# Causal attention scores taken in 512-column pieces through two single PSUM banks by turns

## The reference

```
for i in range(H):                                  # 16 heads, one after the other
    att = jnp.einsum('btd,bsd->bts', q_rot, k_rot) * scale
    if cascade_bias is not None:
        att = att + cascade_w[i - 1] * cascade_bias
    att = jnp.where(causal, -jnp.inf, att)
    att = jax.nn.softmax(att, axis=-1)
    head_outputs.append(jnp.einsum('bts,bsd->btd', att, v[:, i]))
    cascade_bias = jnp.mean(att, axis=1, keepdims=True)
```

## Time and profile before

| | |
|---|---|
| time, median of 3 runs | 3336.99 us (3334.38 to 3339.17) |
| span of the profiled execution | 3451.7 us |
| ACT busy | 3085.3 us, 89% of the span |
| PE busy | 3126.0 us, 91% |
| DVE busy | 2614.4 us, 76% |
| POOL busy | 2147.9 us, 62% |
| first and last "take" on DVE | 46.9 and 3215.3 us |

### The profile page before, as it was taken

One profiled execution on the slowest core, in us unless ns is written; L12 is line 12 of the kernel. 1 busy time (PEld: TensorE's weight loads), 2 busy tenths in 40 slices (PEclk: granted clock), 3 DMA queues, 4 the chain that ended last, 5 costly groups with the idle time before them and its releaser, 6 DMA issues. The chain is left out here.

```text
span 3451.7 us, 93100 instructions
## 1 busy us (share of the span) xinstructions
PE 3126.0 (91%) x29688; PEld 1529.3 (44%) x29688; DVE 2614.4 (76%) x7854; ACT 3085.3 (89%) x8904; POOL 2147.9 (62%) x6194
## 2 busy tenths in 40 slices
PE   6899999989999989998999999998999998898955
PEld 3333333333444434454445444444444543444644
DVE  7666666666877787887888887787888877777754
ACT  4999999999999999998999999998999999888724
POOL 5666666665666367776666677775667655565345
PEclk9999999999999999999999999999999999999986
DMA  5322322232333324343444423344434333344353
GB/s 162 97 86 72 88 71 71 74 88 79 90 101 107 103 78 127 117 122 109 131 115 124 120 84 94 114 116 131 117 93 123 113 101 84 105 121 145 110 187 125
DMA packets 270525, 370.74 MB, mean 107 GB/s; under 512 B 61654, under 2 KB 177118, under 8 KB 270033
## 3 DMA queue, kind: packets, MB, share of 16 engines
q1 hardware_dynamic: 254784, 326.39, 32.4%
q0 software_dynamic: 14976, 37.34, 3.7%
q10 hardware_dynamic: 272, 1.05, 0.1%
HBM read 259.76 MB, written 104.40 MB: 106 GB/s over the span
## 5 line engine op out<-in xcount | busy, mean ns | idle before, releaser
L1490 DVE CUSTOM_DVE_ANT_0 att_a<-scores,window 128x128 f32<-128x128 f32 (+7 forms) x2048 | 1489.6, 754 | 464.9 <-PE scores L1182 307.7
L1356 ACT ACTIVATE att_a<-att_a,neg_max 128x128 f32<-128x128 f32 (+7 forms) x2048 | 1593.0, 778 | 73.3 <-DVE neg_max L1490 69.5
L1366 ACT ACTIVATE att_t<-scores 128x1024 f32<-128x1024 f32 (+7 forms) x2048 | 1329.5, 649 | 88.6 <-PE scores L1200 61.1
L1198 PE MATMUL scores<-q_stack,k_stack 104*128 104x512 bf16 (+3 forms) x3072 | 822.5, 333 | 130.1 <-DVE neg_max L1490 74.7
L1216 PE MATMUL pv<-att_t,v_sb 128*32 128x256 f32 (+7 forms) x16384 | 917.9, 300 | 5.7 <-ACT att_t L1366 3.3
L1182 PE MATMUL scores<-k_stack,q_stack 99*128 99x512 bf16 (+3 forms) x3072 | 687.7, 331 | 67.1 <-ACT att_t L1366 39.1
L1216 PEld LDWEIGHTS pv<-att_t,v_sb 128*32 128x32 f32 x16384 | 328.9, 108 | 592.9 <-issue 549.0
L1198 PEld LDWEIGHTS scores<-q_stack,k_stack 104*128 104x128 bf16 x3072 | 258.4, 98 | 531.2 <-DVE neg_max L1490 233.9
L1200 PE MATMUL scores<-identb,mask 128*128 128x128 bf16 x2048 | 454.7, 222 | 0.0
L1816 POOL TENSOR_SCALAR biasv<-col_sum,w_cas 128x8 f32<-128x8 f32 x240 | 88.8, 370 | 552.9 <-ACT att_t L1366 540.2
L1366 ACT ACTIVATION_READ_ACCUMULATOR att_t<-scores 128x1 f32 x2048 | 424.0, 207 | 0.0
(11 more groups left out here) (345 smaller groups left out, 4342.8 us busy)
## 6 DMA issues: line engine op xcount, KB each, us to landing
runner_r<-in_experts SPq DMA_DIRECT2D x137, 384.0 KB
qk_parts<-of_proj SPq DMA_DIRECT2D x128, 384.0 KB
of_proj<-in_xt SPq DMA_DIRECT2D x29, 1024.0 KB
q_stack<-qk_parts SPq DMA_DIRECT2D x256, 96.0 KB
k_stack<-qk_parts SPq DMA_DIRECT2D x256, 96.0 KB
q_stack<-qk_parts SPq DMA_DIRECT2D x256, 64.0 KB
k_stack<-qk_parts SPq DMA_DIRECT2D x256, 64.0 KB
head_out<-o_sb SPq DMA_DIRECT2D x252, 64.0 KB
```

The source lines that it names most:

```text
L1198: engine.matmul(scores[:, c0:c1], ks[0:ROWS_B, j * P:(j + 1) * P], qs[0:ROWS_B, j * P + c0 - base:j * P + c1 - base], start=True, stop=True)
L1356: engine.activation(taken, taken, EXP, scale=-1.0, bias=neg_max[:, n, i:i + 1], accum_out=row_sum[:, n, i:i + 1]).then_inc(s_exp_a, 1)
L1366: engine.activation(att_t[:, ring:ring + end - base], scores[:, base:end], EXP, accum_out=col_sum[:, n, j:j + 1]).then_inc(s_exp_b, 1)
L1490: engine.tensor_tensor_reduce(out=att_a[:, ring:ring + end - base], in0=scores[:, base:end], in1=window[:, T - (end - base):T], op0=ALU.ad ...
```

## The change

Pass A's rows go through banks 0 and 1 only, in pieces of at most 512 columns that use the two banks by turns. For each pair of blocks (short p, long p+1) there are three pieces: the first 512 columns of the long block, the short block, the rest of the long block. So a unit has 12 pieces (`NP`) where it had 8 blocks. A long block's second piece starts its minimum from the first's result (`scalar=least`), for which DVE waits on its own semaphore. Pass B's short blocks have bank 4 alone, so both cross waits go, in the program and in the planner.

```
+    PIECES, LAST_PIECE = [], {}
+    for p_ in range(0, TB, 2):
+        short_, long_ = A_LONG[p_], A_LONG[p_ + 1]
+        PIECES += [(p_ + 1, 0, WB), (p_, 0, short_), (p_ + 1, WB, long_)]
+        LAST_PIECE[p_], LAST_PIECE[p_ + 1] = len(PIECES) - 2, len(PIECES) - 1
+    NP = len(PIECES)
...
             if kind == "take":
-                busy = cols_a(key[1]) * 1.0417e-3 + 0.078
+                busy = cols_piece(key[1]) * 1.0417e-3 + 0.078
...
-                if p % 2 == 0 and block(x_ - 2, p - 1) >= 0:
-                    yield "exp_b", of_block(block(x_ - 2, p - 1))
...
-                if p % 2:
-                    yield "take", of_block(min(block(u + 2, p - 1), BLOCKS - 1))
...
+        def piece_room(c):
+
+            width = PIECES[c][2] - PIECES[c][1]
+            return scores[:, c % 2 * WB:c % 2 * WB + width]
...
-                pe.wait_ge(s_max, blocks_done(u, p - 2))
-                if p % 2 == 0:
-                    pe.wait_ge(s_exp_b, blocks_done(u - 2, p - 1))
-                for c0 in range(base, end, WB):
-                    c1 = min(end, c0 + WB)
-                    made = engine.matmul(scores[:, c0:c1], qs[0:ROWS_A, i * P:(i + 1) * P],
-                                         ks[0:ROWS_A, c0 - base:c1 - base], start=True, stop=True)
-                made.then_inc(s_a_filled, 1)
+                pe.wait_ge(s_max, pieces_done(u, c - 2))
+                engine.matmul(piece_room(c), qs[0:ROWS_A, i * P:(i + 1) * P], ks[0:ROWS_A, low:high],
+                              start=True, stop=True).then_inc(s_a_filled, 1)
...
                 pe.wait_ge(s_exp_b, blocks_done(u, p - 2))
-                if p % 2:
-                    pe.wait_ge(s_max, blocks_done(u + 2, p - 1))
...
-                dve.wait_ge(s_a_filled, u * TB + p + 1)
+                dve.wait_ge(s_a_filled, pieces_done(u, c))
                 dve.wait_ge(s_exp_a, u * TB + p + 1 - NEG)
+                if low:
+                    dve.wait_ge(s_max, pieces_done(u, c - 2))
                 engine.tensor_tensor_reduce(
-                    out=att_a[:, ring:ring + end - base], in0=scores[:, base:end], in1=window[:, T - (end - base):T],
-                    op0=ALU.add, op1=ALU.min, scale=-1.0, scalar=BIG, accum_out=neg_max[:, n, i:i + 1]).then_inc(s_max, 1)
+                    out=att_a[:, ring + low:ring + high], in0=piece_room(c), in1=window[:, T - A_LONG[p] + low:T - A_LONG[p] + high],
+                    op0=ALU.add, op1=ALU.min, scale=-1.0, scalar=least if low else BIG, accum_out=least).then_inc(s_max, 1)
```

More of the change, by code:

```diff
@@ L317, in cols_a, with cols_piece @@
             return A_LONG[p]
+        def cols_piece(c):
+            return PIECES[c][2] - PIECES[c][1]
         def cols_b(p):
@@ L324, in work @@
             if kind == "fill_a":
-                busy = cols_a(key[1]) * 0.42e-3 + 0.01
+                busy = cols_piece(key[1]) * 0.42e-3 + 0.01
                 return busy, busy + 0.165
@@ L370, in timetable @@
         blocks = [(u, p) for u in range(UNITS) for p in range(TB)]
+        pieces = [(u, c) for u in range(UNITS) for c in range(NP)]
         queues = {
             "ACT": [main],
-            "PE": [[("fill_a", k) for k in blocks], [("fill_b", k) for k in blocks], [("pv", k) for k in blocks],
+            "PE": [[("fill_a", k) for k in pieces], [("fill_b", k) for k in blocks], [("pv", k) for k in blocks],
                    [("rows", x_) for x_ in range(1, UNITS + 1)]],
-            "DVE": [[("take", k) for k in blocks], [("rows_copy", x_) for x_ in range(1, UNITS + 1)],
+            "DVE": [[("take", k) for k in pieces], [("rows_copy", x_) for x_ in range(1, UNITS + 1)],
                     [("o_move", u) for u in range(UNITS)]],
@@ L384, in needs @@
             if kind == "fill_a":
-                x_, p = key
-                if block(*key) >= 2:
-                    yield "take", of_block(block(*key) - 2)
-                if p % 2 == 0 and block(x_ - 2, p - 1) >= 0:
-                    yield "exp_b", of_block(block(x_ - 2, p - 1))
-                if p == 0:
+                x_, c = key
+                if x_ * NP + c >= 2:
+                    yield "take", divmod(x_ * NP + c - 2, NP)
+                if c == 0:
                     hh = head(x_)
@@ L414, in needs @@
             elif kind == "take":
-                x_, p = key
+                x_, c = key
                 yield "fill_a", key
-                if block(*key) >= NEG:
-                    yield "exp_a", of_block(block(*key) - NEG)
-                if p == 0 and x_ >= 2:
+                k = block(x_, PIECES[c][0])
+                if k >= NEG:
+                    yield "exp_a", of_block(k - NEG)
+                if c == 0 and x_ >= 2:
                     yield "lack", x_ - 1
             elif kind == "exp_a":
-                yield "take", key
+                yield "take", (key[0], LAST_PIECE[key[1]])
             elif kind == "exp_b":
@@ L532, in due @@
             elif kind == "take":
[L533 to L538, removed]
+                x_, c = key
+                p = PIECES[c][0]
+                t = start_of(("exp_a", (x_, p))) - HANDOVER
+                if c + 1 < NP:
+                    t = min(t, due("take", (x_, c + 1)) - work("take", (x_, c + 1))[0])
+                if c + 2 < NP:
+                    t = min(t, due("fill_a", (x_, c + 2)) - work("fill_a", (x_, c + 2))[1] - HANDOVER)
             elif kind == "fill_a":
@@ L1169, in fill_a @@
                 qs, ks = q_stack[:, h % 2, slot, :], k_stack[:, h % 2, slot, :]
-                base, end = where("a", p)
+                p, low, high = PIECES[c]
                 i = A_ORDER[p]
-                if p == 0:
+                if c == 0:
                     if u == 0:
@@ L1188, in fill_b @@
                 qs, ks = q_stack[:, h % 2, slot, :], k_stack[:, h % 2, slot, :]
-                base, end = where("b", p)
+                base, end = where(p)
                 j = B_ORDER[p]
```

26 lines of the change are left out of this document (12 added, 14 removed).

## The result

| | before | changed |
|---|---|---|
| time, median | 3338.08 us (3334.38 to 3339.99) | 3369.23 us (3365.61 to 3371.67) |
| ratio | 1 | **1.0093** (95% interval 1.0078 to 1.0107) |
| span of the profiled execution | 3335.4 us (profiled once more) | 3363.8 us |

The change is 31 us slower; the forecast was 46 us faster. One thing must be known first to read any number: the profile shown before the prediction (span 3451.7 us) was 3.4% over the median. Runs 12 to 14 met a chip on which the kernel before takes about 3445 us in every run, and the first profile is of that kind, since it has the same mark: waits put down to "remote", that is, to an event for which the profile names no instruction. Of the first profile,

The account below looks back on a forecast made before the run. ACT was taken as the pacemaker. Terms -80 + 37 - 5 = -48 us of the 3451.7 us profiled span, taken as -46 us of the runs' median: 3337 - 46 = 3291 us; range for 8 in 10, 3220 to 3385 us.

Parts of the forecast that it names:

- Both cross waits go: -80 us: Attention from 1000 us on: ACT regains two thirds of 119.9 us of waits, -80 us; bounds 0 to 133 us.
- PE waiting for L1498 at L1190 for 200 us or more: Sign of a wrong forecast: pass A's fills wait for DVE's takes, ACT waits for L1205 as before; the wait only moved.
- DVE's 4 takes a unit: 0 on the path: 1024 more takes at 0.080 us, 82 us more of DVE, hidden by its idle time: 0 on ACT's path, otherwise 82 us.
- Side work slides: +37 us: After the last pv: 59 tiles instead of 41; 8 late ones cost 30 us, 10 early ones 7 us; between 0 and 67.
- Their leaving frees 5 us: Attention stage: the 18 tiles that leave free ACT of 18 tanh steps and some handovers, -5 us.
- The two-bank loop: 0 on the path: Pass A's fills wait for the take two before; DVE idles 0.4 us a unit; 0 on the path, 100 us as other bound.
- The bounds of the forecast case: Forecast case alone, chance 0.52: 3250 to 3325 us, from gain 40% to all of 133 us and tail 0 to +67.
- the waits only change their name, and the tail is longer: Rival: ACT's idle time comes from side-work bursts on PE, not bank 4; -80 becomes 0, +32 stays: 3368 us, chance 0.14.
- it evens out: Rival: a piece's fill waiting for a take blocks pv and pass B; a third gained, tail takes it: 3337 us, chance 0.08.
- DVE becomes the pacemaker: Rival: extra fixed take costs show on ACT's path, +56 us, nothing regained, tail +37 to +67: 3440 us, chance 0.11.
- the whole gain: Rival: nearly all 133 us come back, tiles mostly fit the finisher's gaps (+15): 3218 us, chance 0.15.
- ACT's two waits near 40 us together: Sign of a right forecast: from 1000 us on, ACT's waits for takes and for L1205 near 40 us instead of 105.

Follow-up runs that it names:

- Runs 12 to 14: Changed kernel without chained piece due dates: plus no pointer operand, 0.9972; plus planner's OVERDUE 4 us instead of 8, 1.0022; kernel before with that OVERDUE, 1.0057.
- run 7: Changed kernel with one cross wait put back, in program and planner (pass B's short fill waits for pass A's short block): 1.0194 to before.
- run 3: Kernel before, banks, waits and order unchanged, but each long block's take done as two instructions (1024 more takes): 1.0040, +13 us.
- run 6: Changed kernel, same order, with the second pieces' minimum starting from a constant instead of the first piece's result: 1.0063 to before.
- 16 and 17: Changed kernel without the planner's rules that make pieces due by the next pieces' dates: 1.0037; the same also without the pointer operand: 0.9999.
- Run 2: Kernel before with the planner starting the tiles of the group before the last late, 59 instead of 41 after the last pv: 1.0126, +42 us.

## Why the prediction was wrong

Term by term, in the order of its sum:

- *"Both cross waits go: -80 us."* **The step that failed.** First its base: two thirds of 119.9 us read from one execution that was 3.4% slower than the timed ones; on a chip of the usual kind the pot was 70.1 us. Then its logic. I counted how far the fills stand ahead in the order (right: DVE now waits 53.9 us for a full ring) and took it that ACT's short waits would be absorbed. They fell by only 13 us, and 21 us came up in other places (POOL's shift chain, tiles, projections), so ACT's idle time stayed at 89 us. The wait for the bank is real, and run 7 prices one of the two at 24 us of the stage, but PE's wait changed its place: two single banks tie pass A's fills to every take, PE is one queue, and its weight loads wait 442.8 us for the fills' banks where they waited 441.9. That this is why ACT gained so little is argued from these rows; no run loosened the two-bank loop alone. The prediction had named such a moved wait under "wrong" in the list of signs ("PE waiting for L1498 at L1190 for 200 us or more"), and L1190 now has 300.4 us of weight loads and 81.7 us of matmuls, with 30.1 us of ACT's waits for L1205 against 32.8.
- *"DVE's 4 takes a unit: 0 on the path."* The price of one was near (70 ns measured against 80), the zero wasn't: 13 us (run 3, with the banks and order of before). And one price was missed: the pointer operand's 60 ns, 50 to 61 us of DVE and about 10 to 13 us of time (runs 6, 16 and 17). Here an idle share of a fifth didn't cover work on an engine for which others wait.
- *"Side work slides: +37 us."* Right in mechanism and near in size: the tail grew by 46 us. Run 2 shows it alone, +53 us of tail, 2.9 us a tile. I let 3.7 us stand for each of the 8 late ones and 0.7 us for each of the 10 early; which of them cost more isn't told apart.
- *"Their leaving frees 5 us."* Too small: 10 us in run 2, and by that it is the greater part of the 18 us by which the last pv came earlier.
- *"The two-bank loop: 0 on the path."* Not measured by itself. It is the other side of the first term: what it costs is already taken off in the 32 to 35 us below.
- *The bounds of the forecast case.* They don't follow from its terms, which added up reach from about 3204 to about 3346 us and not from 3250 to 3325; the 3369 us lie beyond both.

Against the true sum: freer banks about -35 (what is left when run 2's +42 and DVE's +24 are set against +31), DVE +24, slide +42, together +31 us. The first term is a remainder and not a measurement of its own. The stage alone gives much the same: the last pv came 18 us earlier, of which run 2's slide gives 10, and DVE's 24 have to be made good, so 32 are left. Run 7 (24 us of the stage for one of the two waits) is the nearest measurement. Both remainders take it that the prices add and that run 3's 13 us hold in the new order.

Of the rivals, "the waits only change their name, and the tail is longer" (3368 us, chance 0.14) gave the time almost to the microsecond, and that is luck in part: it had the banks and DVE at nothing, where they stand at about -35 and +24, and the bursts of side work that it named as cause aren't shown to be it. The mechanism that the rows bear out is that of "it evens out" (chance 0.08): a piece's fill that waits for a take holds the queue as the cross wait did, and a third of the gain, 27 us, comes; what it lacked were DVE's 24 us and a tail of its full length. "DVE becomes the pacemaker" doesn't hold: ACT's waits for takes fell. Nor does "the whole gain".

The signs listed: 3072 takes with the old slope, L1203 not waiting for DVE, DVE at 86%, 233 us behind the last pv: as said. ACT is above 95% busy, but told nothing: it is 95.8% after, and was 95.8% before on the usual chips. ACT's two waits near 40 us together: they were 56.8. The last pv 80 us earlier: it was 18.

## What to carry to other kernels

Where a planner orders the work, a change of its resources moves side work too; count what stands behind the last step of the main stage before and after, since that count alone (41 to 59 tiles) was worth more than the whole change. Waits of the pacemaker are no estimate of what a freer buffer gives: here the same PE queue that waited for one bank waits for the next, 442.8 us against 441.9. And before a forecast is built on waits of one profile, set its span beside the median of the runs: 3% between them was as large as everything here.

## What the runs showed of the hardware

- A pointer operand in place of a constant as the start value of this DVE reduction lengthens an instruction by 60 ns, at 128 and at 512 columns alike (343 against 285, 745 against 685 ns). DVE's busy time fell by 49 ns for each when it was left out (run 6).
- Chips differ. The medians of the kernel before were 3338 to 3344 us on five occasions and 3445 us on a sixth, on another chip, the runs of each within 0.4%; whether it is the chip or its condition at that time isn't told apart. The same variant stood at 0.9999 on one kind and at 0.9972 on the other. One place where time goes there, in the first profile: the fills end at 2945.93 us as modelled, and the take that needs them starts 3.1 us later, when their semaphore has come.

```profile
2945.27 0.66 PE L1182 MATMUL scores<-k_stack,q_stack 99*128 99x512 bf16 x3 [0.85 <-ACT att_t L1366]
2949.04 0.69 DVE L1490 CUSTOM_DVE_ANT_0 att_a<-scores,window 128x512 f32<-128x512 f32 x1 [3.15 <-remote]
```

What delays them isn't shown; these waits are the "remote" rows, and they make a part of the 116 us between the two profiles' spans.
- ACT's rows can grow without ACT being slower. In run 2, at a place where no tile's work stands beside the attention, they read:

```profile
2901.61 0.86 ACT L1359 ACTIVATE att_a<-att_a,neg_max 128x512 f32<-128x512 f32 x1
2902.22 0.34 ACT L1359 ACTIVATION_READ_ACCUMULATOR att_a<-att_a,neg_max 128x1 f32 x1
2902.32 0.73 ACT L1369 ACTIVATE att_t<-scores 128x512 f32<-128x512 f32 x1
```

and elsewhere, in the second profile of the kernel before:

```profile
1518.37 0.72 ACT L1356 ACTIVATE att_a<-att_a,neg_max 128x512 f32<-128x512 f32 x1
1519.00 0.19 ACT L1356 ACTIVATION_READ_ACCUMULATOR att_a<-att_a,neg_max 128x1 f32 x1
1519.09 0.58 ACT L1366 ACTIVATE att_t<-scores 128x512 f32<-128x512 f32 x1
```

The durations are 0.86 and 0.72 us, but from start to the next operation's start both take 0.71 to 0.72 us. Whoever compares such rows should take the spacing.
